# Softmax row sums moved from an accumulator of ScalarE to products with ones on TensorE, with copies, casts and normalising moved from VectorE to ScalarE

## The chip, the cores and the metric

The kernel runs on one core of one Trainium2 chip. The metric is the device time of one execution in microseconds (us), lower is better. The core has five engines that work side by side, each through its own list of instructions in order: TensorE (PE in the profile, its weight loads PEld), VectorE (DVE), ScalarE (ACT), GpSimd (POOL) and SyncE (SP), which here only issues transfers (DMAs). They wait for one another by counting semaphores.

## The reference, cut to what matters

16 samples are worked on. Each has 256 rows made from an image of 256x256 (two diagonal differences, absolute values, summed, clipped to 0..1) and 77 text rows gathered from a table, so S = 333 rows of D = 256. Then:

```python
h = h + attn(layernorm(h))                     # 16 heads of 16, windows of 128 rows, stride 64
h = h + ffn(layernorm(h))                      # 8 experts, each row goes to its best 2
# in attn, for each window w and head h:
scores = einsum('qd,kd->qk', qw, kw) * scale + pos_bias[h]
probs = softmax(scores, axis=-1)               # exp, divided by its row sum
ow = probs @ vw
merged[window rows] += ow                      # windows overlap; divided by the counts at the end
ctx @ Wo + bo
```

The softmax's row sum, and where it is made, is what the change is about. The value bias bv is added to every value row, so it comes through the softmax unchanged.

## The kernel before, in words

The program has two parts. The first takes the 16 samples one after the other through attention, layer norms and routing, and writes rows sorted by expert to memory. The second (from `run_tiles` on) runs 91 tiles of 128 rows through the experts; the change leaves it alone.

**The first part is a software pipeline written out by hand.** Every engine's program calls `step(b, par)` for b = -2 to 17 (`run_steps`, L233). In step b five samples are in work: sample b is in attention (`att`), b - 1 gets its output product, second layer norm and routing logits (`tail`), b - 2 its places and scatter (`tail2`), b + 1 its projections to queries, keys and values (`proj`), b + 2 its image differences and first layer norm (`inp`). Each step has G = 20 **slots** k = 0 to 19: five windows (NW) times four groups (NG) of four heads. In slot k of a full step,

- TensorE multiplies the scores of group k into `s_bank` (L1026), transposes the probabilities of group k - 3 into `t_bank` (L1040) and multiplies the probabilities of group k - 4 with the values into `o_bank` (L1063), four heads side by side in strips of 32 columns;
- VectorE adds the bias to the scores and takes the minimum of their negative (L757);
- ScalarE takes the exponential of group k - 1 in place, one instruction for each head, whose accumulator gives the row sums (L622, `accum_out`), and copies the transposed group k - 2 from PSUM to `probsT` (L636); for the last group of a window VectorE makes that copy (L772).

After a window's last group VectorE takes the reciprocals of the row sums (L768), spreads each over 16 columns (L776), TensorE transposes that block into `o_bank` (L1072), ScalarE copies it out (L642), VectorE multiplies the window's output by it (L784) and GpSimd adds the result to `ctxT` (L520).

The rest of the work stands at fixed slots between these. Of the projections (`proj`): xn is transposed at k = 0 (L1082) and copied to `xT` (L648); the query and key products are made at k = 2 to 5 (L1104), ScalarE adds their biases in the same slots (L660), VectorE rounds them to bf16 (`part_high`, L733), GpSimd takes the rest (L502), VectorE rounds that (`part_middle`, L738), GpSimd takes the last part (L507). SyncE writes the three parts to memory (`write_part`, L364 to L367) and reads them back as stacks of six slots (`load_stack`, L369 to L373), on which the next step's scores wait (L1021). Value products follow at k = 10 and 11 (L1011), and `add_v` adds bv (L745). Of the `tail`: output product at k = 6 and 7 (L1004), which waits for the last window's `ctxT`; residual (L856), statistics (L706), inverse root on GpSimd at k = 11 (L472 to L484), normalising on VectorE at k = 14 (L714), transposes and gate product at k = 16 and 18 (L1134, L1142). Of `inp`: differences on GpSimd (L533, L536), absolute values on VectorE at k = 7 (L851), sum and clip at k = 11 (L870, L875), statistics at k = 15, inverse root at k = 16, normalising on VectorE at k = 18 (L714), which waits for `rstd1_ready`.

```python
for i, h in enumerate(group_heads(g)):
    seg = probs[:, r, i * WIN:(i + 1) * WIN]
    ins = act.activation(seg, seg, ACT.Exp, bias=neg_max[:, r, i:i + 1], scale=-1.0,
                         accum_out=row_sum[:, (par + v) % 2, h:h + 1])
```

## Time and profile before

| | |
|---|---|
| Median of 3 runs | 1401.03 us (1400.17 to 1402.62) |
| Profiled execution, its own time | 1394.69 us |
| Its span, first to last instruction | 1392.9 us |
| Mean granted TensorE clock | 0.919 |
| Busy: TensorE, VectorE, ScalarE, GpSimd | 85%, 66%, 56%, 44% |
| Start, until the first scores | 0 to 63.4 us |
| Sample 0 | 63.4 to 116.2 us |
| Samples 1 to 15 | 116.2 to about 834 us |
| Experts' tiles | about 870 to 1393 us |

A row of the timeline gives the start, the length, the engine, the line and operation and how many instructions stand in it; in brackets, how long the engine sat idle before it and what released it. Instructions of one engine overlap at their ends, so the time from one start to the next is what an instruction holds its engine for, and the length is how long its result takes. One execution is profiled; its own time lies 6.3 us below the median of the three runs.

### The profile page before, as it was taken

What the parts mean: (1) busy time and instruction counts of PE and PEld (TensorE: products, weight loads), DVE (VectorE), ACT (ScalarE), POOL (GpSimd) and SP (SyncE); (2) the same over time, 40 slices, a digit from 0 to 9 for tenths busy, and PEclk for the clock granted to TensorE, in tenths of its full rate; (3) what the DMA queues carried; (4) which work ended last, traced back from release to release, by engine and by line L of the source; (5) the groups of instructions that cost most, each with busy time, mean ns of one, the idle gap of its engine ahead of it and who ended that gap; (6) DMA issues with size and microseconds to landing.
All of it is one profiled execution on the core that took longest, in us unless ns stands there. A gap on an engine that the chain in (4) does not pass through costs nothing.

```text
span 1392.9 us, 35049 instructions
## 1 busy us (share of the span) xinstructions
PE 1189.1 (85%) x10190; PEld 951.8 (68%) x10191; DVE 920.9 (66%) x4211; ACT 782.9 (56%) x3176; POOL 611.8 (44%) x900
## 2 busy tenths in 40 slices
PE   2386888988988998888889872999999999999996
PEld 1254656655655665555556551999999999999995
DVE  4485989888888889898997864344444444444442
ACT  0196998989899998899899980211111111111110
POOL 5333466565646655665665334122322232232232
PEclk9698899889898988999998985899999999999998
DMA  3694563465357446634643507232233323323222
GB/s 110 133 234 100 109 132 89 95 131 113 88 103 142 92 92 116 128 89 94 133 107 71 96 24 234 36 50 46 49 47 48 49 45 49 48 46 48 46 49 31
DMA packets 98402, 123.36 MB, mean 89 GB/s; under 512 B 15544, under 2 KB 87416, under 8 KB 95192
## 3 DMA queue, kind: packets, MB, share of 16 engines
q1 hardware_dynamic: 75880, 89.96, 30.6%
q0 software_dynamic: 18576, 24.47, 10.9%
q10 hardware_dynamic: 3808, 7.34, 1.8%
q8 instruction: 57, 0.93, 0.3%
q14 instruction: 81, 0.66, 0.2%
HBM read 69.35 MB, written 46.07 MB: 83 GB/s over the span
## 4 chain that ended last, share of the span: by engine, by line
PE 47%; POOL 16%; issue 14%; DMA 12%; ACT 4%; SPq 3%; DVE 3%; POOLq 0%; DVEq 0%; ACTq 0%
PE s_bank L1168 12%; PE t_bank L1168 12%; PE o_bank L1183 11%; DMA qk_parts<-parts_flat 5%; POOL expert_slots L493 4%; DMA expert_slots<-rows,slot_i 4%; DMA stacks<-qk_parts 3%; PE m_bank L1104 3%; ACT probs L622 3%; PE t_bank L1040 2%; SPq L372 2%; POOL rest L502 2%; PE o_bank L1063 2%; POOL parts_flat L507 2%; PE m_bank L1157 1%
## 5 line engine op out<-in xcount | busy, mean ns | idle before, releaser
L622 ACT ACTIVATE probs<-probs,neg_max 128x128 f32<-128x128 f32 x1280 | 497.4, 401 | 21.6 <-DVE neg_max L757 21.0
L757 DVE CUSTOM_DVE_ANT_0 probs<-s_bank,nbias 128x128 f32<-128x128 f32 x1280 | 293.0, 284 | 38.4 <-PE s_bank L1026 36.9
L622 ACT ACTIVATION_READ_ACCUMULATOR probs<-probs,neg_max 128x1 f32 x1280 | 257.4, 201 | 0.0
L1040 PE MATMUL t_bank<-ident,probs 128*128 128x128 f32 x1280 | 221.0, 300 | 28.7 <-ACT probs L622 26.7
L681 ACT ACTIVATE v_all<-s_bank 128x512 f32<-128x512 f32 x91 | 54.4, 598 | 286.9 <-PE s_bank L1168 286.9
L1026 PE MATMUL s_bank<-stacks 96*128 96x128 bf16 x1280 | 136.5, 233 | 68.8 <-DMA stacks<-qk_parts 46.9
L1026 PEld LDWEIGHTS s_bank<-stacks 96*128 96x128 bf16 x1280 | 93.4, 105 | 132.4 <-DMA stacks<-qk_parts 50.7
L1040 PEld LDWEIGHTS t_bank<-ident,probs 128*128 128x128 f32 x1280 | 150.1, 153 | 45.7 <-ACT probs L622 41.7
L636 ACT ACTIVATE probsT<-t_bank 128x512 f32<-128x512 f32 x240 | 141.9, 591 | 57.5 <-PE t_bank L1040 56.7
L1183 PE MATMUL o_bank<-stacks,v_all 128*128 x728 | 172.6, 380 | 0.7 <-issue 0.5
L597 POOL DMA_INDIRECT out_dram<-wq_sb,nbias x46 | 75.7, 1645 | 198.5 <-DVE wq_sb L967 185.3
L1063 PE MATMUL o_bank<-probsT,v_all 128*32 128x128 f32 x2560 | 146.0, 303 | 16.9 <-ACT probsT L636 9.7
L597 POOL DMA_INDIRECT out_dram<-wk_sb,nbias x45 | 73.3, 1629 | 172.8 <-DVE wk_sb L967 170.0
L973 DVE TENSOR_TENSOR v_all<-v_all,t_bank 128x512 f32<-128x512 f32 x91 | 62.6, 688 | 127.1 <-PE t_bank L1168 127.1
L1183 PEld LDWEIGHTS o_bank<-stacks,v_all 128*128 128x128 f32 x728 | 131.3, 190 | 16.0 <-issue 1.8
L675 ACT ACTIVATE v_all<-m_bank 128x256 f32<-128x256 f32 x91 | 35.0, 384 | 143.3 <-PE m_bank L1157 143.3
L493 POOL DMA_INDIRECT expert_slots<-rows,slot_i x96 | 100.0, 1042 | 29.3 <-issue 21.7
L1063 PEld LDWEIGHTS o_bank<-probsT,v_all 128*32 128x32 f32 x2560 | 52.9, 112 | 79.0 <-issue 50.0
L757 DVE DVE_READ_ACCUMULATOR2_ANT neg_max<- 128x1 f32 x1280 | 103.8, 81 | 0.1
L1168 PEld LDWEIGHTS s_bank<-v_all,probs 128*128 128x128 f32 x736 | 91.0, 195 | 3.2 <-ACT v_all L675 0.9
L1168 PE MATMUL s_bank<-v_all,probs 128*128 128x128 f32 x736 | 91.4, 278 | 0.5 <-ACT v_all L675 0.5
L1168 PE MATMUL t_bank<-v_all,probs 128*128 128x128 f32 x736 | 90.7, 277 | 0.0
(158 smaller groups left out, 2079.4 us busy)
## 6 DMA issues: line engine op xcount, KB each, us to landing
stacks<-qk_parts SPq DMA_DIRECT2D x192, 166.5 KB, 5.6
qk_parts<-parts_flat SPq DMA_DIRECT2D x192, 83.2 KB
nbias<-expert_slots SPq DMA_DIRECT2D x91, 129.0 KB, 2.0
w_sb<-in_L_ffn_w_dram ACTq DMA_DIRECT2D x14, 512.0 KB, 5.2
v_all<-v_all SPq DMA_DIRECT2D x64, 96.0 KB, 6.4
x_here<-in_x_dram SPq DMA_DIRECT2D x16, 256.0 KB, 5.7
out_dram<-h_res SPq DMA_DIRECT2D x16, 256.0 KB
stacks<-in_L_ffn_w_dram SPq DMA_DIRECT2D x8, 512.0 KB, 8.5
```

Of the source, the lines that this page charges most:

```text
L493: pool.indirect_dma_start(slots_dram[:, :], bass.IndirectOffsetOnAxis(slot_i[0:n, kk, j:j + 1], 0), rows[0:n, kk, j, :], None).then_inc(sc ...
L597: pool.indirect_dma_start(out[:, :], bass.IndirectOffsetOnAxis(g_rows[r][:, D + 1:D + 2].bitcast(I32), 0), y_sb[r], None, compute_op=ALU.a ...
L622: ins = act.activation(seg, seg, ACT.Exp, bias=neg_max[:, r, i:i + 1], scale=-1.0, accum_out=row_sum[:, (par + v) % 2, h:h + 1])
L636: act.activation(probsT[:, k % 2, :], t_bank[:, k % 2, :], ACT.Copy).then_inc(pT_by_act, 1)
L681: act.activation(hidT[r % 2], s_bank[:, r % 2, :], ACT.Silu).then_inc(silu_ready, 1)
L757: ins = dve.tensor_tensor_reduce(probs[:, r, i * WIN:(i + 1) * WIN], s_bank[:, k % 2, i * WIN:(i + 1) * WIN], nbias[:, h, :], 1.0, BIG, AL ...
L973: dve.tensor_tensor(hidT[r % 2], hidT[r % 2], t_bank[:, r % 2, :], ALU.mult).then_inc(hid_ready, 1)
L1026: mm = pe.matmul(s_bank[:, k % 2, i * WIN:(i + 1) * WIN], q_stack[par][0:KROWS, h, lo:lo + WIN], k_stack[par][0:KROWS, h, lo:lo + WIN], st ...
L1040: mm = pe.transpose(t_bank[:, (k - 3) % 2, i * WIN:(i + 1) * WIN], probs[:, r, i * WIN:(i + 1) * WIN], ident[:, :])
L1063: mm = pe.matmul(o_bank[32 * i:32 * i + 32, vp, (g // 2) * WIN:(g // 2 + 1) * WIN], v_win[bp][:, w, c0:c0 + 2 * HD], probsT[:, (k - 4) % 2 ...
L1168: mm = pe.matmul(bank[:, par, n * P:(n + 1) * P], up_w[par][:, m, a, n * P:(n + 1) * P], gxT[par][:, a * P:(a + 1) * P], start=(a == 0), s ...
L1183: mm = pe.matmul(o_bank[:, r % 2, 0:D], hidT[r % 2][:, a * P:(a + 1) * P], w2_sb[:, bass.ds(e, 1), a, :].rearrange("p o n -> p (o n)"), st ...
```

## The change

Row sums: the exponential loses its accumulator. After the four value products of a group, TensorE makes four more with `sum_of[:, g, :]` (128x32, ones in every fourth column, zeros elsewhere) as the stationary operand and the same `probsT`, into a third block of `o_bank`, accumulated over the window's four groups. VectorE takes the reciprocal of that 128x128 block, and TensorE spreads it with two f32 products with `spread` (for the transposes of `weight`). The spread product, copy and output multiplication of a window stand 2 to 3 slots later than before.

Moves to ScalarE: every `probsT` copy; the first bf16 part (a second activation straight from the product, beside the f32 one); `part_middle`; the value rows (now without bias); absolute values; both normalisings, as scale and shift, for which GpSimd's inverse root makes two more small operations. bv goes through Wo into bo once, before the loop. The prefix and gate products use `m_bank`. SyncE interleaves the writes of the parts with the loads of the stacks, each part with a semaphore of its own. Many slots move by one or two.

```diff
@@ SyncE: parts and stacks
-                    def load_stack(n, dst, slots):
-                        sp.wait_ge(parts_out[n], b1 * PARTS_OUT + PARTS_OUT)
+                    def load_stack(n, t, dst, slots):
+                        sp.wait_ge(parts_out[n][t], (b1 + 1) * PART_OUT)
                         for s, part in enumerate(slots):
...
-                    write_part(0, 0, part1_ready)
-                    write_part(1, 0, part1_ready)
-                    write_part(0, 1, part2_ready)
-                    write_part(0, 2, part3_ready)
-                    write_part(1, 1, part2_ready)
+                    write_part(0, 0, part1_ready, b1 * 4 + 2)
+                    write_part(1, 0, part1_ready, b1 * 4 + 4)
                     if b >= 1:
                         sp.wait_ge(scores_done, (b1 - 1) * G)
-                    load_stack(0, q_stack[par1], Q_SLOTS)
-                    write_part(1, 2, part3_ready)
+                    load_stack(0, 0, q_stack[par1], Q_SLOTS)
+                    write_part(0, 1, part2_ready, b1 * 2 + 1)
+                    load_stack(1, 0, k_stack[par1], K_SLOTS)
+                    write_part(0, 2, part3_ready, b1 * 2 + 1)
+                    load_stack(0, 1, q_stack[par1], Q_SLOTS)
+                    write_part(1, 1, part2_ready, b1 * 2 + 2)
+                    load_stack(0, 2, q_stack[par1], Q_SLOTS)
+                    write_part(1, 2, part3_ready, b1 * 2 + 2)
+                    load_stack(1, 1, k_stack[par1], K_SLOTS)
                     if tail:
                         store_h2()
-                    load_stack(1, k_stack[par1], K_SLOTS)
+                    load_stack(1, 2, k_stack[par1], K_SLOTS)
@@ ScalarE
-                        for i, h in enumerate(group_heads(g)):
+                        for i in range(GH):
                             seg = probs[:, r, i * WIN:(i + 1) * WIN]
-                            ins = act.activation(seg, seg, ACT.Exp, bias=neg_max[:, r, i:i + 1], scale=-1.0,
-                                                 accum_out=row_sum[:, (par + v) % 2, h:h + 1])
+                            ins = act.activation(seg, seg, ACT.Exp, bias=neg_max[:, r, i:i + 1], scale=-1.0)
...
-                    g = (k - 2) % NG
-                    if g != 3 and ((k >= 2 and att) or (k < 2 and tail)):
+                    if (k >= 2 and att) or (k < 2 and tail):
...
-                    v = (k - 4) // NG
-                    if (k - 4) % NG == 3 and ((att and v >= 0) or (tail and v < 0)):
+                    v = (k - 10) // NG
+                    if (k - 10) % NG == 0 and ((att and v >= 0) or (tail and v < 0)):
                         act.wait_ge(weightT_done, b * NW + v + 1)
...
-                    if proj and k == 0:
+                    if proj and k == 1:
                         act.wait_ge(xT_done, b1 + 1)
...
+                    if inp and k == 2:
+                        act.wait_ge(diffs_ready, b2 * 2 + 2)
+                        for d in (diag, anti):
+                            act.activation(d[:, :, :], d[:, :, :], ACT.Abs).then_inc(abs_ready, 1)
-                    if proj and k in (2, 3, 4, 5):
+                    if proj and k in (3, 4, 5, 6):
...
+                        for dst, done in ((qk[:, 2 * n + c, :], qk_ready), (parts[:, 2 * n + c, 0, :], part1_ready)):
+                            act.activation(dst, m_bank[:, c, 0:S], ACT.Identity,
+                                           bias=(bq_col if n == 0 else bk_col)[:, c:c + 1],
+                                           scale=(-SCALE if n == 0 else 1.0)).then_inc(done, 1)
+                    if proj and k == 7:
+                        part_middle(0)
+                    if proj and k == 9:
+                        part_middle(1)
+                    if proj and k == 12:
...
+                        values(0, 0)
+                        values(1, 2)
+                    if proj and k == 13:
+                        values(2, 4)
+                    if tail and k == 15:
...
+                        normalise(h_res[1 - par], rstd2, shift2, lambda j: rows[:, 0, j, 0:D], rows0_ready)
...
+                    if inp and k == 18:
...
+                        normalise(h_in[par], rstd1, shift1, lambda j: xn[:, j, :], xn_ready)
@@ VectorE
-                        dve.tensor_copy(probsT[:, k % 2, :], t_bank[:, k % 2, :]).then_inc(pT_by_dve, 1)
...
-                        dve.tensor_copy(weight[:, vp, :, :], inv_sum[:, vp, :].unsqueeze(2).to_broadcast([P, H, HD]))\
-                            .then_inc(weight_ready, 1)
+                    v = (k - 8) // NG
+                    if (k - 8) % NG == 0 and ((att and v >= 0) or (tail and v < 0)):
...
+                        dve.reciprocal(inv_sum[:, :], o_bank[:, vp, C * WIN:(C + 1) * WIN]).then_inc(inv_ready, 1)
@@ TensorE
+                        for i in range(GH):
+                            mm = pe.matmul(o_bank[32 * i:32 * i + 32, vp, C * WIN:(C + 1) * WIN], sum_of[:, g, :],
+                                           probsT[:, (k - 4) % 2, i * WIN:(i + 1) * WIN],
+                                           start=False, stop=(g == 3), skip_group_check=True)
                         mm.then_inc(pv_done, 1)
...
+                    v = (k - 9) // NG
+                    if (k - 9) % NG == 0 and ((att and v >= 0) or (tail and v < 0)):
+                        pe.wait_ge(inv_ready, b * NW + v + 1)
+                        for c in range(C):
+                            mm = pe.matmul(o_bank[:, (par + v) % 2, (C + c) * WIN:(C + c + 1) * WIN], spread[:, c, :],
+                                           inv_sum[:, :], start=True, stop=True)
...
-                            pe.wait_ge(qk_ready, b1 * 4 + c + 1)
+                            pe.wait_ge(part1_ready, b1 * 4 + c + 1)
...
-                    if tail and k == 6:
+                    if tail and k == 7:
                         pe.wait_ge(ctx_added, b0 * NW + NW)
```

GpSimd: differences both at k = 1, inverse roots at k = 12 and 14, scatters one to a slot from k = 6 to 11, the last parts at k = 8 and 10, window sums at k = 2, 6, 10, 14, 18; before the loop it sets and fills `sum_of` and `spread` (two memsets, three selects).

## Rows read from the trace of the kernel before

**Rows 1.** Busy time by window: PE, PEld, DVE, ACT, POOL, clock, DMA share, GB/s
```profile
300.00:400.00 100.00, 88.30 (x836) 61.04 (x834) 85.82 (x490) 90.74 (x393) 60.01 (x114) 0.90 0.54 110
...
449.20:454.80 5.60, 5.03 (x38) 3.76 (x38) 5.46 (x39) 2.78 (x13) 1.69 (x3) 0.51 0.33 85
```
**Rows 2.** Timeline of PE: starts of samples 1 and 8, and transposes of xn of two samples
```profile
116.21 0.61 PE L1026 MATMUL s_bank<-stacks 96*128 96x128 bf16 x4 [12.46 <-DMA stacks<-qk_parts]
118.19 1.38 PE L1082 MATMUL m_bank<-ident,xn 128*128 128x128 f32 x6
...
449.23 0.61 PE L1026 MATMUL s_bank<-stacks 96*128 96x128 bf16 x4 [2.06 <-DMA stacks<-qk_parts]
740.42 1.37 PE L1082 MATMUL m_bank<-ident,xn 128*128 128x128 f32 x6
```
**Rows 3.** Timeline of PE, sample 7, slots 2 to 12
```profile
407.05 0.40 PE L1026 MATMUL s_bank<-stacks 96*128 96x128 bf16 x4
...
409.50 0.39 PE L1026 MATMUL s_bank<-stacks 96*128 96x128 bf16 x4
...
410.26 0.43 PE L1063 MATMUL o_bank<-probsT,v_all 128*32 128x128 f32 x8
410.62 0.44 PE L1072 MATMUL o_bank<-ident,weight 128*128 128x128 f32 x2
410.89 1.29 PE L1104 MATMUL m_bank<-xT,wq_sb 128*128 128x333 f32 x4
412.01 0.39 PE L1026 MATMUL s_bank<-stacks 96*128 96x128 bf16 x4
...
417.82 1.13 PE L1004 MATMUL m_bank<-wo_sb,ctxT 128*128 128x256 f32 x4
418.79 0.39 PE L1026 MATMUL s_bank<-stacks 96*128 96x128 bf16 x4
...
429.96 0.44 PE L1072 MATMUL o_bank<-ident,weight 128*128 128x128 f32 x2 [1.30 <-DVE weight L776]
...
431.97 0.39 PE L1026 MATMUL s_bank<-stacks 96*128 96x128 bf16 x4
```
**Rows 4.** Timeline of PE, slot 0 of sample 8, after the wait for the stacks
```profile
451.24 0.66 PE L1063 MATMUL o_bank<-probsT,v_all 128*32 128x128 f32 x8 [0.55 <-issue]
451.83 1.38 PE L1082 MATMUL m_bank<-ident,xn 128*128 128x128 f32 x6
```
**Rows 5.** Timeline of ACT, early slots of sample 8
```profile
455.62 0.40 ACT L622 ACTIVATE probs<-probs,neg_max 128x128 f32<-128x128 f32 x1
455.91 0.20 ACT L622 ACTIVATION_READ_ACCUMULATOR probs<-probs,neg_max 128x1 f32 x1
456.00 0.40 ACT L622 ACTIVATE probs<-probs,neg_max 128x128 f32<-128x128 f32 x1
...
461.25 0.59 ACT L636 ACTIVATE probsT<-t_bank 128x512 f32<-128x512 f32 x1
461.72 0.38 ACT L642 ACTIVATE weightT<-o_bank 128x256 f32<-128x256 f32 x1
461.99 0.54 ACT L660 ACTIVATE qk<-m_bank,bq_col 128x333 f32<-128x333 f32 x1
462.41 0.41 ACT L622 ACTIVATE probs<-probs,neg_max 128x128 f32<-128x128 f32 x1
```
**Rows 6.** Timeline of DVE, sample 4, slot 18
```profile
304.00 2.55 DVE L714 TENSOR_SCALAR xn<-h_in,moments,rstd 128x256 f32<-128x256 f32 x3 [2.10 <-POOL rstd L484]
```
**Rows 7.** Groups of instructions, 300 to 700 us; busy us, mean ns, idle before
```profile
L768 DVE RECIPROCAL inv_sum<-row_sum 128x16 f32<-128x16 f32 x42 | 10.4, 248 | 1.2 <-ACT probs L622 1.2
L816 DVE RECIPROCAL score_inv<-score_sum 128x3 f32<-128x3 f32 x9 | 1.6, 176 | 0.3
```
**Rows 8.** Timeline of SP, sample 7: issues of parts and stacks
```profile
430.65 1.22 SPq L366 DMA_DIRECT2D qk_parts<-parts_flat  x2
...
438.98 4.10 SPq L372 DMA_DIRECT2D stacks<-qk_parts  x6
```

More of the change, by code:

```diff
@@ L521, in step @@
                                            ALU.add).then_inc(ctx_added, 1)
+                for k in range(G):
+                    if tail and k == 12:
+                        if b0 >= 1:
+                            pool.wait_ge(rows0_ready, b0 * 3)
+                        pool.wait_ge(ln2_step, b0 * 6 + 6)
+                        inverse_root(moments2, neg_mean2, rstd2, shift2, root2_step, b0, rstd2_ready)
+                    add_window(k)
                     if inp and k == 0:
```

382 lines of the change are left out of this document (180 added, 202 removed).

## The prediction

> **What bounds the kernel now.** I read the page's 40 slices first: about 60% of the span is the loop over samples, the rest start and experts, which the change leaves alone. The loop is even: from the transposes of xn of one sample to those of the thirteenth after it are 622.23 us, so a sample takes 47.86 us [rows 2]. Then busy time by window: ScalarE is busy 90.7%, TensorE 88.3% and VectorE 85.8% of it [rows 1], with none of them full. So I look at what each is held for, start to start, and at the waits.
>
> ScalarE: an exponential with its accumulator holds it 0.38 us, of which the reader of the accumulator is 0.09 (456.00 - 455.91); a 512-column copy 0.47, a 256-column copy 0.27, an activation of 333 columns with a bias pointer 0.42 [rows 5]. A sample has 80 exponentials (30.4), 15 copies of 512 (7.1), 5 of 256 (1.35), two of 666 (0.60 each by the slope of 0.8 ns a column between 256 and 512: 1.2), 4 biased ones (1.7) and 0.1 of small work: 41.8 us. The busy share gives 43.4 (0.907 x 47.86), since the last instruction before a gap counts whole.
>
> TensorE: scores, transposes and value products of a slot hold it 1.12 us (409.50 to 410.62), 22.4 a sample; to that come the transposes of `weight` (0.27, five times), four projections of 1.12, six 256-column products of 0.97, and about 2.1 of transposes and gate (half of 1.38 each at full clock [rows 4]) [rows 3]: 36.1 us. So neither engine's work fills 47.86. What fills it, by halves: slots 2 to 11 took 24.92 us (407.05 to 431.97), with 22.3 of TensorE's work (11.2 + 4.5 + 5.8 + 0.8) [rows 3], and the other ten 22.9, with 21.0 of ScalarE's (15.2 of exponentials, 8 copies 3.8, the rest 2.0). Together 43.3, and **4.6 us of waits**: for VectorE, whose spreading copy held TensorE up 1.30 us [rows 3], whose normalising sat 2.10 us in wait for GpSimd and then took 2.55, with the next scores queued behind it [rows 6]; for the stacks, 2.06 us [rows 2]; and for a clock of 0.51, the lower of the two levels (1.2 of 2.4 GHz), after that wait [rows 1].
>
> **The change, part by part.** Each per sample.
>
> *ScalarE* gives up 80 readers, 7.2 us. I take it that the exponential alone is 0.29 (455.91 - 455.62) [rows 5]; a 128-column copy without a pointer would be 0.17 by the slope, a bound that reads 10 us better. It takes 5 copies (5 x 0.47 = 2.35), 4 more biased ones (1.7), two of 666 (1.2), three value rows (0.8), absolute values (2 x 0.47 = 0.9) and six normalisings. One pointer adds 0.09 (0.42 against 0.33 for 333 columns by the slope), so two on 256 columns make 0.45: 2.7. Sum 9.7, net **+2.5**: 44.3 by starts, 45.9 by the busy share. The Trainium skill, "ScalarE: Activation LUTs", section "What ACT_TABLE_LOAD costs", has each pointer at about 93 ns and an overlap of 93 ns, by which an exponential is an estimated 0.29 and a normalising 0.49; the rows agree within 0.04. [...]
>
> *VectorE* gives up copies, spreads, casts, value rows, absolute values and normalisings and gets five reciprocals of 128 columns. No row has one from PSUM; by 248 ns for 16 columns and 176 for 3 it is 5.5 ns a column, 0.86 us [rows 7]. I cost it at nothing: it stands in slot 0, 4, ... and TensorE reads it a slot later. VectorE falls far below the other two. Its waits of the last paragraph go; next late is ScalarE.
>
> *TensorE* gets 8 records to a slot (4 heads, f32 as two). The same 8 for the values hold it 0.36 (410.26 to 410.62) [rows 3] and 0.59 at half clock (451.24 to 451.83) [rows 4]. So 0.23 scales with the clock, 0.13 does not. Going by the 8 records as they stand, the sums cost 0.36 a slot, 7.2; if the fixed part is paid once per strip pattern, 0.23, 4.6. I take 0.23, because two sets of the same strips follow each other, and keep 0.36. The Trainium skill, "TensorEngine Tiling (Array Packing)", section "Key Properties", says that changing the tiling mode drains the engine; that is a reading of the 0.13 and leads to the lower price. Spread products: two f32 of 128 columns for 0.27 of transposes; four records of 256 columns take 0.97, so 0.49, +1.1. TensorE's work: 36.1 + 4.6 + 1.1 = **41.8** (up to 44.4).
>
> *New waits on ScalarE* in slots 2 to 11. ScalarE's iteration j copies group j - 2, which TensorE transposes in its slot j + 1. What it does behind that copy comes after TensorE's value and sum products (0.36 + 0.23 = 0.59).
> - Slot 4: the key product waits for `part1_ready`, moved from iteration 2 to 3: copy 0.47, f32 activation 0.42, bf16 one 0.54 to its end = 1.4, less 0.59: 0.8. Slot 5 the same, less the spread product 0.49: 0.3.
> - Slot 2: xT, moved from iteration 0 to 1: 0.47 + 0.7 - 0.59 = 0.6.
> - Slot 7: output product waits for `ctxT`, whose window is now closed in slot 6 instead of 4: copies 0.47 + 0.38, VectorE's multiplication about 0.4, GpSimd's addition about 0.8 (both by their 256 columns; no row here bounds them better than 0.3 and 0.9) = 2.1, less 0.59: 1.5.
>
> Sum 3.3 us (bounds 0 and 4.5). Queued behind these on TensorE are the next scores and transposes, on which ScalarE's next copy waits, so in this half they count.
>
> *Halves after.* Slots 2 to 11: 10 x 1.35 + 4.5 + 5.8 + 1.0 + 3.3 = 28.1, by TensorE. The other ten: 10 x (4 x 0.29 + 0.47) = 16.3, normalisings 2.7, values 0.8, window copies 0.5, x2T 0.6 = 21.0, by ScalarE. Waits of VectorE and for the stacks gone; TensorE's lag of up to a slot can be worked off in the second half (-1), and as much I leave for what is not seen (+1). **49.1 us a sample, +1.2; for samples 1 to 15, +18.**
>
> *SyncE* issues the same 24 transfers, but now waits for six landings instead of two. From the end of the last write's issue to the first load were 7.1 us (431.87 to 438.98), for writes queued behind six loads [rows 8]; interleaved the queue is shorter, and after the last landing one load stands instead of six (4.10 us of issue), so -3 there against +2 for parts that come a slot later. Nothing on the path, if the landings shorten.
>
> *Start and sample 0.* Five GpSimd operations before the loop (0 to 4 us; the slowest nearby row has 0.85 each [rows 6]), against normalising on ScalarE (-1): 0. Sample 0 ends in 12.46 us of waiting for stacks [rows 2], so its longer work is hidden; its six landings are not: +1 (-6 to +8). *After the loop*: two more small GpSimd steps on the last sample's path, +1; experts 0.
>
> Sum: 18 + 1 + 1 = +20 on the profiled execution's 1394.69 (span 1392.9, 1.8 around it), 1414.7. The median lies 6.3 above that execution, so +20 on 1401.03 is **1421 us**. A measurement here can tell about 0.2%, 2.8 us.
>
> **Rivals.**
> - *The waits of VectorE were worth more than the new ones* (faster; 0.32). The new waits overlap: ScalarE catches up in them, and the loop runs by ScalarE's 45.9 us with the clock up. -2.0 x 15 = -29, 1372. For it: VectorE's waits and the 0.51 clock are seen, the new ones only argued. Against: TensorE's first half is 24.8 even without them, the second 21.0, 45.8 in all with no wait anywhere. It decides at 3.3 us of new waits: below 2.1 it wins.
> - *The landings in series* (slower; 0.12). If each wait stays at 7.1 us, the last load is issued 7.1 - 3.4 (five loads less) + 2 = 5.7 later, less the about 1.5 that a single load lands sooner: a sample of about 52, +62, 1463. Against: the bunches that make 7.1 are gone.
> - *Even* (0.08): new waits of 2.1, 1401.
> - *The reader hid nothing* (0.03): an exponential alone holds ScalarE 0.38. 7.2 more, over +100.
> - *Forecast* (0.45): 1421, by itself 1408 to 1445, the upper end from sums at 0.36 (+2.6 a sample in all, half of it in TensorE's half).
>
> **How the numbers follow.** Faster takes its rival and a sliver of the forecast's doubt on the waits: 0.34; same 0.08; slower 0.58. The range reaches from the faster rival's time to 1452, which leaves out the landings in series and the far end of the first.
>
> **What would show it.** Right: mean of an exponential unchanged near 0.40, starts 0.29 apart; value and sum products of a slot about 0.59 start to start; TensorE idle in slots 4, 5 and 7, released by ScalarE's bf16 parts and by `ctxT`; VectorE under 70%; xn transposes 49 us apart; stack waits gone. Wrong: no such idle time and 46 us a sample (the first rival); idle time before the first scores of every sample (landings); sum products at 0.36 or more.

## The result, and the profile of the changed kernel

The changed kernel takes **1594.82 us** (median of four runs, 1593.18 to 1598.52) against 1401.21 us for the kernel before beside it: ratio 1.1385, 95% interval 1.1362 to 1.1407. Forecast were 1421 us and a range of 1372 to 1452, so the sign was right and the size far off: 194 us slower where 20 were expected. The profiled execution has a span of 1591.4 us, 198.5 more than before.

The page of the kernel after, its first line and part 1:

```profile
span 1591.4 us, 39136 instructions
PE 1296.7 (81%) x12914; PEld 1062.3 (67%) x12915; DVE 778.9 (49%) x3814; ACT 837.3 (53%) x2248; POOL 610.3 (38%) x969
```

No engine became the bound: all of them are busy for a smaller share than before. The loop alone is longer. The transposes of xn, one of the first things of a sample, start here:

```profile
236.75 0.78 PE L1095 MATMUL m_bank<-ident,xn 128*128 128x128 f32 x6 [0.29 <-ACT xn L657]
...
912.19 0.77 PE L1095 MATMUL m_bank<-ident,xn 128*128 128x128 f32 x6 [0.29 <-ACT xn L657]
```

Eleven samples lie between the two: (912.19 - 236.75) / 11 = **61.40 us a sample**, where before it was 47.86 [rows 2]. 13.54 more, 15 times, is 203 us; the start gives about 5 of it back.

Busy time from 300 to 700 us, of before (first line) and after ([rows 1] has only its first 100 us for before), and of two short stretches of after; columns as in [rows 1] (time, then PE, PEld, DVE, ACT and POOL with their counts, granted clock, DMA share, GB/s):

```profile
300.00:700.00 400.00, 347.79 (x3306) 238.64 (x3305) 351.56 (x1978) 359.26 (x1553) 237.16 (x412) 0.90 0.52 107
300.00:700.00 400.00, 314.47 (x3641) 228.53 (x3640) 220.31 (x1368) 300.37 (x833) 179.56 (x329) 0.91 0.35 81
427.50:437.40 9.90, 7.80 (x48) 5.02 (x52) 3.70 (x29) 3.25 (x10) 1.32 (x2) 0.67 0.01 2
471.90:475.00 3.10, 3.01 (x23) 2.65 (x27) 0.93 (x8) 1.53 (x6) 2.35 (x11) 0.50 0.69 208
```

ScalarE, which was to be nearly full, is busy 75% of the time and VectorE 55%. So the added time is mostly waiting, and the list of waits of 300 to 700 us says which (waiting engine, its operation, what it waited for: total us, times, longest):

```profile
ACT probsT L679 <- PE t_bank L1048: 97.9, 71, 3.6
DVE head_out L824 <- ACT weightT L685: 96.3, 32, 3.8
DVE probs L807 <- PE s_bank L1037: 81.0, 47, 2.4
PE m_bank L1104 <- DVE taken L845: 16.1, 7, 2.3
PE m_bank L1121 <- DVE region_end L855: 14.5, 7, 2.1
PE m_bank L1151 <- ACT rows L657: 11.5, 6, 1.9
PE m_bank L1121 <- ACT parts_flat L710: 8.9, 14, 1.0
PE m_bank L1015 <- POOL w_sb L547: 11.0, 4, 2.8
```

Read the first three together: ScalarE's copy waits for TensorE's transposes, VectorE's output multiplication for ScalarE's copy of the spread weights, and VectorE's minima for TensorE's scores. **That is a ring in which every engine waits for another**, and no row of the page's busy shares can show it. TensorE's timeline over the sample that starts at 420.93 (start, length, tile, count, idle time before it and its releaser):

```profile
422.66 0.42 PE L1066 MATMUL o_bank<-probsT,v_all 128*32 128x128 f32 x8
422.90 0.40 PE L1072 MATMUL o_bank<-probsT,sum_of 128*32 128x128 f32 x8
423.28 0.71 PE L1080 MATMUL o_bank<-inv_sum,spread 128*128 128x128 f32 x4
...
427.53 0.20 PE L1104 MATMUL m_bank<-taken,before 128*128 128x24 bf16 x1 [2.29 <-DVE taken L845]
...
433.81 2.28 PE L1121 MATMUL m_bank<-xT,wq_sb 128*128 128x333 f32 x4 [2.07 <-DVE region_end L855]
...
438.92 1.39 PE L1121 MATMUL m_bank<-xT,wk_sb 128*128 128x333 f32 x4 [0.90 <-ACT parts_flat L710]
...
449.26 1.13 PE L1015 MATMUL m_bank<-wo_sb,w_sb 128*128 128x256 f32 x4 [2.75 <-POOL w_sb L547]
...
471.99 1.37 PE L1151 MATMUL m_bank<-ident,rows 128*128 128x128 f32 x6 [1.91 <-ACT rows L657]
...
478.04 1.33 PE L1158 MATMUL m_bank<-gate_sb,rest 128*128 128x8 f32 x12 [0.73 <-ACT rest L734]
```

With the small ones that are not shown (0.33, 0.35, 0.35, 0.65, 0.17, 0.29), TensorE waits 12.8 us in this sample. Its work at the full clock turned out to be 43.6 us (below, `five_again`). The 5.0 left of 61.4 is put down to time at the lower clock, as a remainder: in the two windows above the granted clock is 0.67 and 0.50, right behind the waits for `taken` and `rows`, and a query product there holds TensorE 2.36 us (427.66 to 430.02 in the timeline) where the key product at 438.92 holds it 1.23. The stacks are no part of it: SyncE issues the last load of a sample's parts at 529.6, and the scores that read them start at 544.5 without a wait.

How the ring closes, on VectorE, one sample later (its timeline):

```profile
485.52 2.67 DVE L830 TENSOR_TENSOR below_best<-best 128x24 f32<-128x24 f32 x1
...
493.62 0.42 DVE L824 TENSOR_TENSOR head_out<-o_bank,weightT 128x256 f32<-128x256 f32 x1 [3.70 <-ACT weightT L685]
...
495.01 0.16 DVE L855 TENSOR_TENSOR region_end<-region_end,m_bank 128x8 f32<-128x8 f32 x1
```

and on ScalarE at the same time:

```profile
492.71 0.60 ACT L679 ACTIVATE probsT<-t_bank 128x512 f32<-128x512 f32 x1 [3.56 <-PE t_bank L1048]
493.21 0.38 ACT L685 ACTIVATE weightT<-o_bank 128x256 f32<-128x256 f32 x1
...
498.99 0.60 ACT L679 ACTIVATE probsT<-t_bank 128x512 f32<-128x512 f32 x1 [3.10 <-PE t_bank L1048]
```

The copy of the spread weights into `weightT` stands in ScalarE's iteration 10 + 4v (2, 6, 10, 14, 18 of a sample), and VectorE multiplies by it in its slot of the same number. In the kernel before, the copy stood one iteration ahead of its use (`(k - 4) % NG == 3` on ScalarE, with the multiplication one slot later). The change moved the copy by three slots and the multiplication by two. ScalarE's iteration k begins with a copy of what TensorE transposes in its slot k + 1. So in each of these slots VectorE, which could run ahead, waits for ScalarE, which waits for TensorE; queued behind VectorE's multiplication are the next minima and, in slot 2, `place` and `region_end`, which TensorE waits for.

### The profile page after: what moved, and what is told of

Read it like the earlier page. It is cut to its first block, busy times and chain, and to the rows that moved or that the text cites. A ratio compares the mean times of both kernels' runs of the same rounds, so it can differ in the third digit from the quotient of the medians.

```text
span 1591.4 us, 39136 instructions
## 1 busy us (share of the span) xinstructions
PE 1296.7 (81%) x12914; PEld 1062.3 (67%) x12915; DVE 778.9 (49%) x3814; ACT 837.3 (53%) x2248; POOL 610.3 (38%) x969
## 4 chain that ended last, share of the span: by engine, by line
PE 55%; issue 17%; DVE 9%; ACT 8%; DMA 4%; POOL 4%; SPq 1%; POOLq 0%; ACTq 0%; DVEq 0%
PE s_bank L1184 10%; PE t_bank L1184 10%; PE o_bank L1199 10%; PE t_bank L1048 5%; DVE probs L807 3%; PE m_bank L1015 3%; PE m_bank L1121 3%; DMA qk_parts<-parts_flat 3%; PE s_bank L1037 3%; ACT probs L667 2%; PE o_bank L1066 2%; DVE below_best L830 2%; PE o_bank L1080 2%; PE m_bank L1022 2%; ACT rows L657 2%
## 5 line engine op out<-in xcount | busy, mean ns | idle before, releaser
L667 ACT ACTIVATE probs<-probs,neg_max 128x128 f32<-128x128 f32 x1280 | 407.5, 399 | 12.2 <-DVE neg_max L807 12.1
L679 ACT ACTIVATE probsT<-t_bank 128x512 f32<-128x512 f32 x320 | 189.9, 594 | 237.0 <-PE t_bank L1048 234.6
L1048 PE MATMUL t_bank<-ident,probs 128*128 128x128 f32 x1280 | 214.8, 295 | 6.4 <-ACT probs L667 4.3
L1037 PEld LDWEIGHTS s_bank<-stacks 96*128 96x128 bf16 x1280 | 100.9, 106 | 86.2 <-issue 39.1
L824 DVE TENSOR_TENSOR head_out<-o_bank,weightT 128x256 f32<-128x256 f32 x80 | 33.9, 424 | 231.7 <-ACT weightT L685 231.7
L1072 PE MATMUL o_bank<-probsT,sum_of 128*32 128x128 f32 x2560 | 134.8, 281 | 0.0
L527 POOL TENSOR_TENSOR rest<-qk,parts_flat 128x666 f32<-128x666 f32 x32 | 45.1, 1409 | 132.8 <-ACT qk L710 124.3
L1121 PE MATMUL m_bank<-xT,wq_sb 128*128 128x333 f32 x128 | 71.3, 707 | 29.5 <-DVE region_end L855 26.8
```

Of the source, the lines that this page charges most:

```text
L679: act.activation(probsT[:, k % 2, :], t_bank[:, k % 2, :], ACT.Copy).then_inc(pT_ready, 1)
L1037: mm = pe.matmul(s_bank[:, k % 2, i * WIN:(i + 1) * WIN], q_stack[par][0:KROWS, h, lo:lo + WIN], k_stack[par][0:KROWS, h, lo:lo + WIN], st ...
L1048: mm = pe.transpose(t_bank[:, (k - 3) % 2, i * WIN:(i + 1) * WIN], probs[:, r, i * WIN:(i + 1) * WIN], ident[:, :])
L1072: mm = pe.matmul(o_bank[32 * i:32 * i + 32, vp, C * WIN:(C + 1) * WIN], sum_of[:, g, :], probsT[:, (k - 4) % 2, i * WIN:(i + 1) * WIN], st ...
L1121: mm = pe.matmul(m_bank[:, c, 0:S], (wq_sb if n == 0 else wk_sb)[:, a, c * P:(c + 1) * P], xT[:, a, :], start=(a == 0), stop=(a == C - 1))
```

## The experiments

Times are medians, ratios those to the kernel before on the same chip, with 95% intervals. "After" is the changed kernel.

### The copy of the spread weights

**copy_slot9**, one edit of after:

```diff
-                    v = (k - 10) // NG
-                    if (k - 10) % NG == 0 and ((att and v >= 0) or (tail and v < 0)):
+                    v = (k - 9) // NG
+                    if (k - 9) % NG == 0 and ((att and v >= 0) or (tail and v < 0)):
                         act.wait_ge(weightT_done, b * NW + v + 1)
```

> ScalarE's copy of a window's spread reciprocals stands in its slot 9 of the window instead of 10, nothing else. Theory of the closed ring (VectorE in slot k waits for a copy that ScalarE makes in its own slot k, which stands behind a transpose that TensorE makes in its slot k + 1, which stands behind VectorE's slot k): the wait of head_out (96 us in 400) goes, the wait for ctxT in slot 7 falls from 2.75 us to under 0.7, the wait for region_end in slot 3 from 2.07 to under 0.5, and the half clock after it goes; 6 us a sample, 1505 us. Rival, the added work of TensorE and ScalarE itself sets the time: the waits move elsewhere, 1585 to 1600.

1508.31 us, ratio 1.0773 (1.0714 to 1.0831): 87 us less than after. VectorE's wait for the copy fell from 96.3 us to the first line here (waits, 300 to 700 us), and TensorE's largest are now those of ScalarE's side work:

```profile
DVE head_out L824 <- ACT weightT L685: 11.9, 24, 1.0
PE m_bank L1151 <- ACT rows L657: 14.9, 7, 2.4
PE m_bank L1104 <- ACT xT L691: 10.4, 7, 1.6
PE m_bank L1121 <- ACT parts_flat L710: 9.8, 15, 1.2
```

**before_copy_late** puts the same fault into the kernel before, and nothing else of the change:

```diff
-                    v = (k - 4) // NG
-                    if (k - 4) % NG == 3 and ((att and v >= 0) or (tail and v < 0)):
+                    v = (k - 5) // NG
+                    if (k - 5) % NG == 3 and ((att and v >= 0) or (tail and v < 0)):
                         act.wait_ge(weightT_done, b * NW + v + 1)
```

> The kernel before with one edit: ScalarE's copy of the window's weights stands one slot later, in the slot in which VectorE's output multiplication waits for it, as in the changed kernel. Theory: this alone closes the ring, five times a sample, and costs 2 to 5 us a sample, 1430 to 1475 us. Rival, the ring needs the changed kernel's other late work too: within 10 us of 1400.

1490.37 us, ratio 1.0671 (1.0645 to 1.0697), 93 us more than before and more than expected. Its waits of 300 to 700 us, and below them the same two in the kernel before:

```profile
DVE head_out L784 <- ACT weightT L642: 65.5, 37, 2.8
ACT probs L622 <- DVE neg_max L757: 51.8, 49, 2.6
```

```profile
DVE head_out L784 <- ACT weightT L642: 6.7, 14, 0.6
ACT probs L622 <- DVE neg_max L757: 14.5, 21, 1.2
```

This position is worth about 90 us in either kernel as it stands, and the second has no ones-products at all.

### Other members of the ring

**taken_slot0** moves VectorE's chain to `taken` a slot earlier, away from GpSimd's differences of the image.

```diff
-                    if tail2 and k == 1:
+                    if tail2 and k == 0:
                         if b9 >= 1:
                             dve.wait_ge(score_e_ready, b9)
```

> VectorE's routing chain (below_best to taken) back in slot 0, nothing else. Theory: in slot 1 its first operation took 2.67 us instead of 0.17 because GpSimd's two differences run then, and TensorE waits 2.29 us for taken; in slot 0 the operation takes under 0.7 and the wait goes, 2.3 to 4 us a sample, 1535 to 1560 us. Rival, the added work sets the time: 1585 to 1600.

1599.52 us, ratio 1.1424 (1.1334 to 1.1514), the same as after within the intervals: a miss. The chain came to stand beside the same two GpSimd operations with another of its members (VectorE's timeline):

```profile
429.06 0.13 DVE L830 TENSOR_TENSOR below_best<-best 128x24 f32<-128x24 f32 x1
...
429.60 2.94 DVE L842 TENSOR_SCALAR onehot<-onehot,text_ok 128x16 f32<-128x16 f32 x1
```

**diffs_later** moves the other side instead: GpSimd's differences and ScalarE's absolute values.

```diff
# GpSimd
-                    if inp and k == 1:
+                    if inp and k == 2:
                         pool.wait_ge(x_in, b2 * 64 + 64)
# ScalarE
-                    if inp and k == 2:
+                    if inp and k == 3:
                         act.wait_ge(diffs_ready, b2 * 2 + 2)
```

> The kernel after, with one edit: GpSimd's two differences of the image and ScalarE's two absolute values of them stand one iteration later (2 and 3 instead of 1 and 2). In the kernel after, one 24-column operation of VectorE takes 2.67 us while the two differences run, and TensorE waits 2.29 us for `taken` behind it. Theory (the collision of the two engines is one of the waits of the ring): below_best falls to about 0.17 us, TensorE's wait for `taken` goes below 0.5, a sample is 2 to 2.5 us shorter, 1555 to 1570 us. Rival (another wait of the same slot takes its place, as where the chain of VectorE was moved instead): 1585 to 1605.

1599.36 us, ratio 1.1432 (1.1401 to 1.1464): the rival. below_best takes 0.18 us, and TensorE's wait for `taken` is gone. Others took its place (waits, 300 to 700 us), 8.5 us for `xT` and 5.9 more for the biased parts:

```profile
PE m_bank L1104 <- ACT xT L691: 8.5, 7, 1.3
PE m_bank L1121 <- ACT parts_flat L710: 14.8, 10, 2.0
PE m_bank L1121 <- DVE region_end L855: 14.5, 7, 2.1
```

VectorE, done with `taken` at 489.06 here, still waits 3.78 us for `weightT` (its timeline):

```profile
488.02 0.18 DVE L830 TENSOR_TENSOR below_best<-best 128x24 f32<-128x24 f32 x1
...
493.72 0.42 DVE L824 TENSOR_TENSOR head_out<-o_bank,weightT 128x256 f32<-128x256 f32 x1 [3.78 <-ACT weightT L685]
```

So the collision is seen, but taking it away alone gives nothing back in this ring.

**qk_slots2to5** gives ScalarE's biased copies of the query and key projections back the iterations they had before.

```diff
-                    if proj and k in (3, 4, 5, 6):
-                        n, c = (k - 3) // 2, (k - 3) % 2
+                    if proj and k in (2, 3, 4, 5):
+                        n, c = (k - 2) // 2, (k - 2) % 2
...
-                        act.wait_ge(qk_done, b1 * 4 + k - 2)
+                        act.wait_ge(qk_done, b1 * 4 + k - 1)
```

> ScalarE's eight biased activations back in slots 2 to 5 (from 3 to 6), nothing else. Theory: TensorE's waits for the bf16 parts in slots 4 and 5 (0.90 and 0.33 us) go, 1 to 2 us a sample, 1565 to 1580 us. Rival, ScalarE's work sets the time: within 5 us of 1595.

1588.28 us, ratio 1.1344 (1.1311 to 1.1377): 6.5 us less, where 15 to 30 were expected, and not clear of after's interval. TensorE's waits for the biased parts, 8.9 us of 300 to 700 in after, are gone, and no other wait of TensorE grew by more than 1.1. But the granted clock of that window is 0.87 instead of 0.91, and TensorE is busy 326.1 us of the 400 instead of 314.5. So most of what the waits gave back went into a lower clock; why it fell, no run shows.

### Slots set right

**five_earlier** puts five things on ScalarE one iteration earlier: copy_slot9's edit, qk_slots2to5's edit, and

```diff
# the copy into xT
-                    if proj and k == 1:
+                    if proj and k == 0:
...
# the second normalising, into rows
-                    if tail and k == 15:
+                    if tail and k == 14:
...
# the copy into x2T
-                    if tail and k == 17:
+                    if tail and k == 16:
```

> The copy of copy_slot9, and with it ScalarE's other side work one slot earlier, where the kernel before had it: xT in slot 0, the biased activations in 2 to 5, the second normalising in 14, x2T in 16. Theory (TensorE waits in its slot k for work that ScalarE does in its slot k - 1, behind a copy that itself waits for TensorE's slot k): the waits left in copy_slot9 (rows 2.37, xT 1.54, rest 1.01, bf16 parts 0.98 and 0.33, region_end 0.39, ctxT 0.26 us) go, 5 to 7 us a sample, 1400 to 1435 us. Rival, work sets what is left (TensorE's 44 us with the sums, ScalarE's 45): no more than 2 us a sample, 1480 or more.

**1386.79 us**, ratio 0.992 (0.9883 to 0.9957), below the 1400 to 1435 expected; one of its four runs, a stray of 5541.71 us, stands in the median and not in the ratio. The same kernel once more, as **five_again**:

> The kernel of five_earlier once more, for its interval: 1380 to 1392 us, a ratio of 0.985 to 0.996 to the kernel before. Rival, its gain was chance: an interval that holds 1.

1383.49 us (1382.37 to 1385.07), ratio 0.9905 (0.9888 to 0.9922). A sample takes 47.40 us (two starts of xn transposes), and the window of 300 to 700 us is

```profile
300.00:700.00 400.00, 367.81 (x4786) 272.56 (x4778) 289.28 (x1797) 385.00 (x1091) 233.75 (x432) 1.00 0.46 105
```

ScalarE is busy 96% of it: 0.9625 x 47.40 = 45.6 us of work a sample, TensorE 0.92 x 47.40 = 43.6, and the clock is not lowered at all.

**side_work_earlier** is five_earlier without the move of the `weightT` copy.

> The side work of five_earlier without the copy: the window's output copy stays in slot 10. Theory: the ring through VectorE stays closed and holds slots 1 to 7, so most of copy_slot9's 87 us stays lost: 1520 to 1560 us. Rival, the copy's slot was only worth what ScalarE could not do in time: under 1480 us.

1543.37 us, ratio 1.1049 (1.0974 to 1.1125), 51 less than after. The copy alone is worth 87 us, the rest alone 51, both together 208: 70 of these come only when neither is left.

### What the two ways of summing cost

**sums_twice** issues every ones-product twice into the same sums (added to after); the sums come out doubled, so the weights, and all that follows of them, are halved.

```diff
+                        for i in range(GH):
+                            mm = pe.matmul(o_bank[32 * i:32 * i + 32, vp, C * WIN:(C + 1) * WIN], sum_of[:, g, :],
+                                           probsT[:, (k - 4) % 2, i * WIN:(i + 1) * WIN],
+                                           start=False, stop=(g == 3), skip_group_check=True)
```

> The changed kernel with each of the products with ones issued twice, so that the sums and with them the output's weights are off by two. Theory: another 0.22 to 0.34 us a slot on TensorE; in the slots where TensorE waits behind them for another engine (2, 3, 4, 5, 7, 16, 18) it hides, in the other 13 it counts: 3 to 4 us a sample, 1640 to 1660 us. Rival, TensorE's work sets the time everywhere: 4.6 to 7 us a sample, 1665 to 1705 us. If the ones-products cost next to nothing: within 10 us of 1595.

1584.97 us, ratio 1.1347 (1.1257 to 1.1437), 10 less than after, which is not clear of noise (the interval holds after's 1.1385): twice the products cost nothing, where 45 to 65 us were expected. TensorE's waits get shorter by them (`taken` 2.29 to 1.93, `w_sb` 2.75 to 2.32), and the profiled clock is 0.935 instead of 0.921.

**five_sums_twice** is the same edit on five_earlier, and halves the weights as well.

> The five moves (measured at 1383.5), with every ones-product issued twice into the same sums; the weights come out halved, so all that follows of them is off by two. Prices TensorE's share of the idea where the waits are gone. 0.24 us a slot is 4.8 us a sample; TensorE is busy 91.9% of 47.4 us, 43.6, and would need 48.4. Theory (the ones-products cost their own length once TensorE is as near to its limit as ScalarE): 1 to 4 us a sample, 1400 to 1450 us. Rival (as in the kernel after, where doubling cost nothing): 1378 to 1390.

1408.6 us (1404.82 to 1412.55), ratio 1.0071 (1.0048 to 1.0093), 25 more than five_again. A sample takes 48.75 us (xn transposes at 410.99 and 459.74), and TensorE is now the full engine:

```profile
300.00:700.00 400.00, 389.00 (x5983) 299.65 (x5986) 281.08 (x1743) 374.36 (x1059) 231.29 (x447) 1.00 0.47 109
```

0.9725 x 48.75 = 47.4 us of work, 3.8 more than with the products once: 0.19 us a slot. Once the slots are right they do count, by 1.35 us a sample; the other 2.4 of the 3.8 fit into the 3.8 us a sample in which TensorE was idle in five_again.

**with_accumulator** adds the accumulators of before to after's exponentials; nothing reads what they give.

```diff
-                        for i in range(GH):
+                        for i, h in enumerate(group_heads(g)):
                             seg = probs[:, r, i * WIN:(i + 1) * WIN]
-                            ins = act.activation(seg, seg, ACT.Exp, bias=neg_max[:, r, i:i + 1], scale=-1.0)
+                            ins = act.activation(seg, seg, ACT.Exp, bias=neg_max[:, r, i:i + 1], scale=-1.0,
+                                                 accum_out=row_sum[:, ((k - 1) // NG) % 2, h:h + 1])
```

> The changed kernel with its accumulators put back on all 1280 exponentials (their results are not used): 0.09 us each, 7.2 us of ScalarE's work a sample. Theory (waits in a ring set the time, ScalarE is idle a third of it): the readers fall into ScalarE's idle time, up to 2 us a sample, 1595 to 1625 us. Rival, ScalarE's work sets the time: 7 us a sample, 1695 to 1710 us.

1626.95 us, ratio 1.1648 (1.1549 to 1.1747): 32 us more than after, 2.1 a sample, at the upper end of what was expected.

**five_with_accumulator** is the same edit on five_earlier.

> five_earlier with the accumulators back on the exponentials (results not used). Theory: ScalarE now bounds, so its 7.2 us a sample count in full, where they cost 2 us in the changed kernel: 1490 to 1510 us. Rival, ScalarE still has idle time for them: under 1430.

1475.17 us, ratio 1.0562 (1.0508 to 1.0616), 92 more than five_again, 6.1 for each of 15 samples; the expected 1490 to 1510 counted the readers in full. ScalarE's 45.6 us and 7.2 for 80 readers make 52.8; from one start of the xn transposes to the next are 52.45 (384.92 to 437.37). The window, with ScalarE busy 98.4%:

```profile
300.00:700.00 400.00, 350.25 (x4251) 256.97 (x4248) 254.31 (x1591) 393.49 (x1561) 215.07 (x414) 0.94 0.46 103
```

### SyncE's order

**sync_as_before** gives after the queue order of before: five writes of parts, three loads, the last write, three loads.

```diff
...
                     write_part(1, 0, part1_ready, b1 * 4 + 4)
-                    if b >= 1:
-                        sp.wait_ge(scores_done, (b1 - 1) * G)
-                    load_stack(0, 0, q_stack[par1], Q_SLOTS)
                     write_part(0, 1, part2_ready, b1 * 2 + 1)
-                    load_stack(1, 0, k_stack[par1], K_SLOTS)
                     write_part(0, 2, part3_ready, b1 * 2 + 1)
-                    load_stack(0, 1, q_stack[par1], Q_SLOTS)
                     write_part(1, 1, part2_ready, b1 * 2 + 2)
-                    load_stack(0, 2, q_stack[par1], Q_SLOTS)
+                    if b >= 1:
+                        sp.wait_ge(scores_done, (b1 - 1) * G)
+                    load_stack(0, q_stack[par1], Q_SLOTS)
                     write_part(1, 2, part3_ready, b1 * 2 + 2)
-                    load_stack(1, 1, k_stack[par1], K_SLOTS)
                     if tail:
                         store_h2()
-                    load_stack(1, 2, k_stack[par1], K_SLOTS)
+                    load_stack(1, k_stack[par1], K_SLOTS)
```

`load_stack` itself, not shown, waits for all three parts here and then issues its six loads.

> SyncE writes and loads in the order of the kernel before (two waits for landings instead of six), nothing else. Theory of the closed ring: the stacks land some 9 us before they are needed, so the loop is unchanged, within 8 us of 1595. Rival, landings in series hold the loop: faster by over 20 us.

1633.7 us, ratio 1.1668 (1.1633 to 1.1704): 39 us slower, outside both forecasts.

**five_sync_as_before** has the same edit on five_earlier.

> The five moves (measured at 1383.5), with SyncE's writes of the parts and loads of the stacks in the order of the kernel before: five writes, then three loads, the last write, three loads. In the kernel after the same edit cost 39 us. Theory (what it cost there were writes and loads in one bunch that disturbed waits of the ring, not a late landing): 1383 to 1393 us. Rival (the landings come later in the sample, and with samples of 47.4 instead of 61.4 us they meet the first scores): stack waits of 1 us or more a sample appear, 1400 to 1430 us.

1442.84 us, ratio 1.0332 (1.0309 to 1.0355), 59 more than five_again. This is outside both as well: above the rival's 1400 to 1430, and not in its place, since the waits for stacks are 3.2 us in all of 300 to 700, 0.4 a sample. Two things are late instead. The first stands behind the loads in SyncE's queue, the next sample's image and text index (timeline of SyncE's queue, then of GpSimd):

```profile
406.66 1.21 SPq L372 DMA_DIRECT2D qk_parts<-parts_flat  x2
...
415.49 2.82 SPq L379 DMA_DIRECT2D stacks<-qk_parts  x6
...
423.26 0.34 SPq L353 DMA_DIRECT2D text_idx<-in_x_txt_dram  x1
```

```profile
429.44 1.06 POOL L558 DMA_INDIRECT w_sb<-in_L_txt_weight_dram,text_idx  x1 [3.95 <-DMA text_idx<-in_x_txt_dram]
```

The last loads wait 6.6 us (408.89 to 415.49) for the last write's landing, GpSimd then 3.95 us for the index. But in sync_as_before, 39 us slower than after, GpSimd never waits for the index, so that is not what the two have in common.

The second is in both: the second normalising. TensorE's wait for `rows` is 19.4 us in eight samples (five_again 5.7), and in sync_as_before 17.9 in six (after 11.5). ScalarE itself stands still before it, 12.7 us in eight samples, and never in five_again. By the program the normalising waits for the landing of an earlier sample's six scatters (L727 in after). The last of them, and the normalising:

```profile
406.58 0.97 POOL L513 DMA_INDIRECT expert_slots<-rows,slot_i  x1 [0.31 <-issue]
```

```profile
415.01 1.58 ACT L653 ACTIVATE rows<-h_res,shift,rstd 128x256 f32<-128x256 f32 x3 [1.43 <-issue]
```

GpSimd is not late here. ScalarE gets to the normalising 6.7 to 7.0 us after the last scatter's issue, in eight samples, and has to wait until 7.9 to 9.2 us after it; in five_again it comes 6.2 us after it (430.40 and 436.64) and need not wait. So the scatters land later. From 406.6 to 415.0 the DMA engines are busy 93% of the time, in the same stretch of five_again (430.4 to 436.6) 72%. That the bunch of writes and loads holds up the scatters is read from these numbers; no run isolates it. The 1.7 us a sample that `rows` adds are less than half of the 4.0 by which a sample got longer. The rest, of which a lower clock (0.96 instead of 1.00 from 300 to 700 us) is a part, is open.

### Versions that beat both

**five_abs_vector** is five_earlier with the absolute values back on VectorE, where before had them (slot 7).

```diff
# ScalarE
-                    if inp and k == 2:
-                        act.wait_ge(diffs_ready, b2 * 2 + 2)
-                        for d in (diag, anti):
-                            act.activation(d[:, :, :], d[:, :, :], ACT.Abs).then_inc(abs_ready, 1)
# VectorE, slot 7
+                        dve.wait_ge(diffs_ready, b2 * 2 + 2)
+                        for d in (diag, anti):
+                            bits = d[:, :, :].bitcast(I32)
+                            dve.tensor_scalar(bits, bits, 0x7FFFFFFF, None, ALU.bitwise_and).then_inc(abs_ready, 1)
                         dve.wait_ge(abs_ready, b2 * 2 + 2)
```

> five_earlier with the absolute values back on VectorE (slot 7, as the kernel before had them). Theory: with the ring open ScalarE is busy 96% of the loop and is what bounds it, so its 1.0 us less a sample comes back as time: 1368 to 1378 us, a ratio near 0.98. Rival, it is held by waits of TensorE (rows, xn, taken, 0.7 us each): within 4 us of five_earlier.

**1379.47 us** (1378.86 to 1381.5), ratio 0.9875 (0.9856 to 0.9895), the lowest of all, 4 us under five_again, where the theory had 1378 at most and the rival no more than 4 us. Of ScalarE's 0.9 us a sample about 0.3 reached the time; ScalarE is still busy 94.8%, and TensorE's waits are the same, which speaks for the rival.

**five_abs_diffs_later** adds diffs_later's edit of GpSimd to it.

> The five moves with the absolute values back on VectorE (measured at 1379.5), and GpSimd's two differences one iteration later, 2 instead of 1. There TensorE waits 0.70 us a sample for `taken`, behind a VectorE operation of 2.14 us, and ScalarE is 95% busy. Theory (ScalarE bounds, but this wait is still passed on to it): 0.3 to 0.7 us a sample, 1369 to 1376 us. Rival (ScalarE's work covers the wait): within 3 us of 1379.5.

1383.12 us, ratio 0.9895 (0.9878 to 0.9913). The theory's gain did not come: the medians lie 3.6 us apart the other way, just outside the rival's 3, and the intervals of the two ratios overlap. TensorE no longer waits for `taken`, and its wait for `region_end` rises from 3.5 to 5.1 us in nine samples.

## Why the forecast was right in its sign and wrong in its size

**The step that failed** is the one on VectorE: "VectorE falls far below the other two. Its waits of the last paragraph go; next late is ScalarE." The first sentence held: 55% busy. The second did not. (The reciprocal, "I cost it at nothing", nearly was nothing: TensorE waits for it 1.1 us in all of 300 to 700.) The change also moved ScalarE's `weightT` copy into the slot in which VectorE uses it, and I priced that wait neither for itself nor for what is queued behind it; "Waits of VectorE and for the stacks gone" put both at nothing. It is 96.3 us in 6.5 samples, 14.8 us a sample, the largest wait of VectorE's, and it is the slack that VectorE had ahead of ScalarE. copy_slot9 (-87) and before_copy_late (+93) show its price from both sides. A low busy share was taken for freedom to wait.

**New waits on ScalarE** were forecast at 3.3 us, all in slots 2 to 11, and the second half was summed without any. Slot 4 was 0.8 and came out 0.90, slot 5 0.3 and 0.33, slot 7 1.5 and 2.75; slot 2, priced 0.6 for `xT`, waits 2.29 for `taken`, and 1.3 for `xT` once that is taken away (diffs_later). `region_end` (2.07), `rows` (1.91) and `rest` (0.73) were not on the list, though `rows` and `rest` stood by the same rule one iteration too late. Waits of TensorE came to 12.8 us, and beside them 5.0 that are put down to the lower clock, for which no term stood. side_work_earlier (-51) and the five moves together (-208) show that such waits don't add: each is counted as far as the others leave it.

**The sign** was forecast for a reason that is a part of the true one. The waits in slots 4, 5 and 7 are there, 4.0 of the 12.8 us, and positions on ScalarE did decide. But the position that cost most was in no term, and with all five set right the sign turns (0.9905).

**What held.** An exponential without its accumulator holds ScalarE 0.29 (four in 1.17), its mean unchanged at 0.399. Value and sum products of a slot take 0.62 us to the next product (422.66 to 423.28), 0.59 forecast; the spread 0.55, 0.49 forecast. The price of the ones-products, 0.23 a slot, is 0.26 by these rows (0.62 less the 0.36 of the values alone in [rows 3]), and a further set costs 0.19 by five_sums_twice, so the upper bound of 0.36 is out. ScalarE's work, 45.9 us by the busy share, measures 45.6. TensorE's 41.8, added up from starts, measures 43.6 by the busy share. The reciprocal is 0.95, 0.86 forecast. **The faster rival** ("ScalarE catches up in them, and the loop runs by ScalarE's 45.9 us with the clock up", 1372) is not what this kernel does, but with five positions changed it comes within 12 us: 1383.5 and 47.4 us a sample. Its condition, new waits below 2.1 us, was the right one, and it failed on positions, not on work.

**Landings.** "Nothing on the path" was right for after: no stack waits from 300 to 700 us. But the reordered queue is worth 39 us there and 59 with the slots right. The prediction looked only at who waits for the stacks. With the writes and loads in bunches, others wait for landings: the second normalising for the scatters, in both kernels, and in one of them GpSimd for the next sample's text index. I named neither.

**The start** was put at 0 and gave about 5 us: the first xn transposes stand at 58.59, before at 63.83. It was not looked into.

**The change taken apart.** With the slots right, the whole change, sums and moves together, is worth 13 us against before (ratio 0.9905). Leaving the accumulators out is worth 92, against a kernel that has both them and the ones-products; what the moved copies and casts are worth by themselves, with the sums still made by the accumulator alone, no run shows. As delivered, the positions cost 211 (1594.8 against 1383.5).

## What to carry to other kernels

When work moves between engines that run in a ring of slots, write down for each moved item the slot in which it is made, the slot in which it is used, and what its maker waits for first; an item made and used in the same slot takes away the lead of the engine that uses it, however idle that engine looks. Price such waits together, by what is queued behind each, since one that is removed alone is often replaced by its neighbour (taken_slot0, diffs_later, qk_slots2to5) and the same edits pay in full only together. When transfers are put in another order, list everyone who waits for a landing, in other queues and for the next sample too, and not only those who wait for the transfers that were moved.

## What the runs showed of the hardware that I had not expected

**A short VectorE operation can stand still while GpSimd computes.** A 24-column operation of 0.17 us (below_best before: 171 to 183 ns, 16 times) takes 2.6 to 2.7 us in 12 samples of after; in the last four, where GpSimd has no more differences to make, it takes 0.12 to 0.18. GpSimd's timeline beside the VectorE rows above:

```profile
486.00 1.10 POOL L568 TENSOR_TENSOR diag<-x_here,x_below 128x512 f32<-128x512 f32 x1
487.04 1.09 POOL L570 TENSOR_TENSOR anti<-x_below,x_here 128x512 f32<-128x512 f32 x1
```

It ends at 488.19, with the second of them (488.13), and GpSimd's two are not stretched (1.10 us in before too). Moved apart in diffs_later it takes 0.18. The Trainium skill, "SBUF — State Buffer", section "SBUF: two separate sides", says that a VectorE operation with two inputs in SBUF and a GpSimd operation that reads SBUF lock a shared port pair exclusively, that whichever starts first has it for its whole instruction, and that the other "fully blocks". The rows agree that VectorE is blocked and GpSimd is not. They differ in two points: VectorE's record starts 0.5 us ahead of the first difference, and it is held through two GpSimd instructions, not one. GpSimd's gather, which runs from 484.91 to 485.97 when VectorE's record starts, is not what holds it: in diffs_later the operation starts at the same point of the gather (0.61 us in) and takes 0.18.

**More TensorE work can cost nothing.** With all ones-products doubled, after ran no longer (10 us less, within the noise) at a clock of 0.935 instead of 0.921; on the kernel without those waits the clock from 300 to 700 us is 1.00 with or without them, and they cost 25 us.

**The lower clock comes back with the waits, but not with each of them.** From 300 to 700 us the granted clock is 0.91 in after and 0.90 in before, but 1.00 in five_again, with TensorE busy 92%. So a part of what the five moves gain comes with the clock. It is not the ring alone that lowers it (before has none), nor does every wait: in after the clock is 0.67 behind the waits of 2.29 and 2.07 us and 0.50 behind that of 1.91, but 1.00 from 446.5 to 461.0, behind the longest, 2.75 us.
